# A graph layer on one core: one shared edge stream of split rows, and three node groups summed through a counted adjacency

## What is computed

```python
agg = segment_sum(x[src], dst, num_segments=6250)          # 200000 edges, rows of 256 floats
h = relu(agg @ W_rel + b_rel + x @ W_root)                 # 6250 x 512
gates = h @ W_ih.T + b_ih + b_hh                           # i, f, g, o; f is not used
c = sigmoid(i) * tanh(g)
out = layernorm(x + (sigmoid(o) * tanh(c)) @ W_fc + b_fc)  # 6250 x 256
```

## Time and profile before

| what | value |
|---|---|
| median of 3 runs | 1966.54 us (1962.2 to 1970.02) |
| profiled execution, span (the page gives no other time for it) | 2818.8 us |
| its mean granted clock of TensorE | 0.800 |
| PE busy, weight loads busy | 1874.5 us (66%), 1404.0 us (50%) |
| POOL busy, DVE busy, ACT busy | 1505.5 us (53%), 627.4 us (22%), 333.4 us (12%) |
| software queue of the gathers | 184.11 MB, 22.4% of 16 engines |
| steps gathered, pair steps counted | 345, 92 |

### The profile page before, as it was taken

How to read it: one execution, slowest core, us unless ns; L and a number is a source line. 1 busy time by engine, 2 the same in 40 slices (tenths; PEclk the granted TensorE clock), 3 DMA queues, 4 the chain that set the end, 5 groups by cost and what they waited for, 6 DMA issues and landing times.

```text
span 2818.8 us, 31563 instructions
## 1 busy us (share of the span) xinstructions
PE 1874.5 (66%) x7122; PEld 1404.0 (50%) x7123; DVE 627.4 (22%) x1236; ACT 333.4 (12%) x650; POOL 1505.5 (53%) x1774
## 2 busy tenths in 40 slices
PE   3736684857576757568568668568655765675678
PEld 0324262534445646457457457346534654554457
DVE  7411422323231211112012112112111211121112
ACT  0000020101010101001001112001101110111013
POOL 5776447364545474555654544654565547446640
PEclk9767696778778877789679789679778877887789
DMA  4333113121212232232222222322232223222220
GB/s 155 89 95 92 57 57 89 45 85 52 76 54 87 73 103 75 76 87 86 83 85 84 72 71 67 90 74 70 75 89 74 74 60 97 67 70 83 86 67 15
DMA packets 103600, 217.34 MB, mean 77 GB/s; under 512 B 37253, under 2 KB 56760, under 8 KB 103480
## 3 DMA queue, kind: packets, MB, share of 16 engines
q0 software_dynamic: 67392, 184.11, 22.4%
q10 hardware_dynamic: 32984, 25.63, 3.1%
q1 hardware_dynamic: 3202, 7.33, 0.7%
HBM read 210.58 MB, written 6.40 MB: 77 GB/s over the span
## 4 chain that ended last, share of the span: by engine, by line
PE 47%; another core or an unknown queue 26%; issue 17%; DVEq 4%; DVE 4%; ACT 1%; ACTq 0%; DMA 0%; SPq 0%
PE ps_blk L396 18%; PE ps_agg L339 16%; PE ps_y L405 3%; PE ps_blk L381 3%; PE ps_blk L383 3%; PE ps_win L320 2%; DVEq L694 1%; DVE hot_key L682 1%; DVEq L678 1%; DVE onehot L694 1%; PE ps_win L329 1%; PE ps_tr L320 1%; DVEq L690 0%; PE ps_tr L369 0%
## 5 line engine op out<-in xcount | busy, mean ns | idle before, releaser
L285 POOL DMA_INDIRECT rows<-in_x,idx x1404 | 1417.2, 1009 | 1171.6 <-issue 1098.1
L339 PE MATMUL ps_agg<-rows,onehot 128*125 x2760 | 784.4, 443 | 605.5 <-DVE onehot L694 419.3
L339 PEld LDWEIGHTS ps_agg<-rows,onehot 128*125 128x125 f32 x2760 | 580.0, 218 | 805.9 <-issue 704.6
L396 PE MATMUL ps_blk<-h_t,wih_sb 128*128 128x250 f32 x2400 | 581.1, 403 | 194.1 <-issue 115.4
L396 PEld LDWEIGHTS ps_blk<-h_t,wih_sb 128*128 128x128 f32 x2400 | 491.1, 206 | 283.7 <-issue 128.4
L694 DVE SCALAR_TENSOR_TENSOR onehot<-iota_f,tile_first,dst_f 128x500 f32 x345 | 255.4, 740 | 1276.3 <-remote 727.0
L702 DVE TENSOR_TENSOR tanh_g<-sig_i,tanh_g 128x250 f32<-128x250 f32 x100 | 42.0, 420 | 651.6 <-ACT tanh_g L507 516.2
L486 ACT ACTIVATE agg_n<-ps_agg 125x512 f32<-125x512 f32 x24 | 14.3, 597 | 1200.1 <-PE ps_agg L361 516.5
L320 PE MATMUL ps_win<-hot_key,hot_lo 128*128 x248 | 113.6, 610 | 38.5 <-DVE hot_key L682 29.2
L271 POOL COPY idx<-src_sb 128x4 int32 x352 | 81.9, 233 | 65.0 <-issue 62.8
L682 DVE TENSOR_TENSOR hot_key<-iota_h,rel 128x1960 f16 x92 | 107.8, 1171 | 0.8 <-issue 0.8
(11 more groups left out here) (106 smaller groups left out, 645.4 us busy)
## 6 DMA issues: line engine op xcount, KB each, us to landing
rows<-in_x,idx POOLq DMA_INDIRECT x1404
hot_key<-in_xb ACTq DMA_DIRECT2D x7, 896.0 KB
x_t<-in_xT ACTq DMA_DIRECT2D x50, 125.0 KB
x_n<-in_x ACTq DMA_DIRECT2D x50, 125.0 KB
out<-y ACTq DMA_DIRECT2D x50, 125.0 KB
wih_sb<-in_w_ihT SPq DMA_DIRECT2D x1, 2048.0 KB
wih_sb<-in_w_ihT SPq DMA_DIRECT2D x1, 1024.0 KB
src_sb<-in_srcT SPq DMA_DIRECT2D x1, 786.0 KB, 6.7
```

Of the source, the lines that this page charges most:

```text
L285: g.indirect_dma_start(rows[:, k * QC + j, :], None, x, bass.IndirectOffsetOnAxis(ap=idx[:, k, j:j + 1], axis=0)).then_inc(landed[k][j // ...
L339: last = mm(o, onehot[:, half * QC + j, :], rows[:, ds(slot + j, 1), :], start=False, stop=False)
L396: last = mm(o, wih_sb[:, k, col:col + P], h_t[:, k, :], start=(k == 0), stop=(k == KH - 1))
```

## The change

- **Split rows.** A prologue on DVE and SP cuts each value of `x` into a high part (low 12 bits cleared) and the rest, and writes both to a table `x_parts` in HBM, 2 KiB a row, in 10 pieces of 625 nodes. The gather reads this table. `rows` and `onehot` become float32r, and a visit multiplies 512 columns at once (high and low side by side in one PSUM bank); ACT copies the low half and DVE adds the high half (`copy_low`, `add_high`). POOL starts only when all 10 pieces are written; 5 splits stand among the first 5 windows on DVE.
- **One stream.** Tiles are taken in node order and share steps: a tile begins with the step on which the last one ended (a further **visit** of it, no further gather). By the drawn edges there are 258 steps and 301 visits in 44 tiles.
- **Ring** of 6 steps in place of 13; BANKS 3 in place of 4.
- **Three dense groups.** The first 750 nodes are counted: 75 windows with, by the drawn edges, 92 + 50 + 47 = 189 pair steps, three products of 7 batches with two `xs` buffers.
- **Order.** Five windows (37 pair steps) come before the first tile; the other 70 stand in 27 portions of 2 or 3 windows, behind the gates of j = 0, 1 and 2 (9 of the turns); the second tile comes between the gates j = 1 and j = 2; a product batch stands ahead of a gate group. On DVE a portion's windows stand ahead of the LSTM multiplies of that gate group. Turns 5, 11 and 17 have no tile.

```diff
+DENSE = 3
+EARLY_WINDOWS = 5
+HEAD_TURNS = ((3, 2, 2), (3, 2, 2), (2, 2, 2))
+WINDOW_TURNS = ((3, 3, 3), (3, 3, 2), (3, 3, 2))
+PERIOD = 6
-RING = 13
+RING = 6
-BANKS = 4
+BANKS = 3
...
-        rows = sb("rows", [P, RING * QC, D_IN])
-        onehot = sb("onehot", [P, 2 * QC, TN])
+        rows = sb("rows", [P, RING * QC, D_ROW], f32r)
+        onehot = sb("onehot", [P, 2 * QC, TN + 1], f32r)
...
+            for i in range(2):
+                pool.wait_ge(piece_out[i], 16 * X_PIECES // 2)
...
                     pool.wait_ge(steps_summed, s + 1)
                     for j in range(QC):
                         g.indirect_dma_start(
-                            rows[:, k * QC + j, :], None, x,
+                            rows_f[:, k * QC + j, :], None, x_parts,
...
+            def visit(o, s, u, half, first=False):
+                pe.wait_ge(gathered, s + (RING + 1))
+                pe.wait_ge(hot_ready, u + 1)
+                for j in range(QC):
+                    ins = mm(o, onehot[:, half * QC + j, 0:TN], rows[:, ds(slot + j, 1), :].squeeze(1), start=(first and j == 0), stop=False)
+                    if j == 0 and not first:
+                        ins.then_inc(steps_summed, 1)
+                ins.then_inc(hot_used, 1)
...
                 if t is not None:
+                    tile_sum(t, 0)
+                for j in range(KH):
+                    if j == 2 and t is not None:
+                        tile_sum(t, 1)
+                    if j in at:
+                        product_batch(k, at[j])
+                    if not first:
+                        gates(n - 1, j)
+                    if j < 3 and wins[j] > 0:
+                        windows(w, wins[j])
+                        w = w + wins[j]
...
+            def split(i):
+                dve.wait_ge(piece_in[i % 3], 16 * (i // 3) + 16)
+                if i >= 2:
+                    dve.wait_ge(piece_out[i % 2], 16 * (i // 2))
+                link(v.tensor_scalar(x_out[i % 2][:, :, 0, :].bitcast(i32), x_in[i % 3].bitcast(i32), HIGH_BITS, None, ALU.bitwise_and))
+                v.tensor_tensor(x_out[i % 2][:, :, 1, :], x_in[i % 3], x_out[i % 2][:, :, 0, :], ALU.subtract).then_inc(piece_split, 1)
...
+            def visit(t, s, u, half, first):
+                dve.wait_ge(hot_used, u + (2 if first else 1))
+                v.scalar_tensor_tensor(onehot[:, 0:QC, 0:TN] if first else onehot[:, ds(half * QC, QC), 0:TN],
...
+            def add_high(t, a):
+                dve.wait_ge(low_copied, t + (a + 1))
+                v.tensor_tensor(agg_n[:, a, :], ps_agg[a][0:TN, 0:D_IN], agg_n[:, a, :], ALU.add).then_inc(agg_evac, 1)
...
+            for i in range(EARLY_WINDOWS):
+                window(i)
+                split(5 + i)
+            first_visit(0)
```

More of the change, by code:

```diff
@@ L555, in _ @@
-            n = HEAD_TURN
-            turn(n, head, tail(n - 1), tail(n - 2))
-            turn(n + 1, tail(n), head, tail(n - 1), t=n)
-            turn(n + 2, tail(n + 1), tail(n), head, t=n + 1)
-            with act.Fori(HEAD_TURN + 3, GROUPS) as n:
-                turn(n, tail(n - 1), tail(n - 2), tail(n - 3), t=n - 1)
+            act.wait_ge(gate_bias_ready, 1)
+            windows(0, EARLY_WINDOWS, 0)
+            w = EARLY_WINDOWS
+            for n, wins in enumerate(HEAD_TURNS):
+                g = DENSE + n
+                turn(n, g, g - 1 if n >= 1 else None, g - 2 if n >= 2 else None, t=2 * n, w=w, wins=wins, node=w * WN)
+                w += sum(wins)
@@ L565, in _ @@
-            gates(n - 1)
+            store(n - 2, n - 2)
+            for j in range(KH):
+                gates(n - 1, j)
             deviation(n - 1)
-            store(n - 1, tail(n - 2))
-            act.wait_ge(y_free, 32 * GROUPS + 16)
+            store(n - 1, n - 1)
+            act.wait_ge(y_free, 16 * GROUPS)
         @block.vector
@@ L741, in normalise, with windows, turn @@
                 ins.then_inc(out_ready, 1)
-            def turn(n, back=2, t=None, begun=False, w=None, begin=None):
-                if begin is not None:
-                    tile_sum(begin, 0)
+            def windows(w, n_windows):
+                for i in range(n_windows):
+                    window(w + i if isinstance(w, int) else dve.snap(w + i, min_val=0, max_val=WINDOWS - 1))
+            def turn(n, back=2, t=None, w=None, wins=(0, 0, 0), end=False):
                 if t is not None:
-                    if back == 0:
-                        windows(w)
-                    if not begun:
-                        tile_sum(t, 0)
-                    if w is not None and back > 0:
-                        windows(w)
-                    tile_sum(t, 1)
+                    other_visits(t)
+                    first_visit(t + 1)
@@ new lines, in turn @@
+                if t is not None:
+                    other_visits(t + 1)
+                    if not end:
+                        first_visit(t + 2)
+                    add_high(t, 1)
+                if wins[2] > 0:
+                    windows(w + (wins[0] + wins[1]), wins[2])
+                if back >= 1:
+                    cell(n - 1, 2)
+                    out_gate(n - 1, 1)
+                    cell(n - 1, 3)
+                    out_gate(n - 1, 2)
+                    out_gate(n - 1, 3)
+                    norm_stats(n - 1)
```

695 lines of the change are left out of this document (397 added, 298 removed).

## The result

The changed kernel takes 2135.5 us (median of 4, 2133.9 to 2142.7) against 1965.6 (1962.2 to 1970.0) for the kernel before: a ratio of **1.087** (95% interval 1.085 to 1.090), slower. Forecast were 2010, 2.2% slower, and a range of 1890 to 2130: the side was right, the size was not, and the range was missed by 5.5 us.

A forecast was written before the change was run, and what follows sets the result against it. It took POOL's descriptors to bound the kernel from turn 5 on, PE and DVE counting before. PE's new work, 1868 us, plus 105 of row waits and 35 of clock gave 2008, predicted as 2010, 2.2% slower; range 1890 to 2130.

The forecast's parts named there:

- The turn of the bound: Whole kernel: 87 steps, 470 us, leave POOL's chain, more than PE's waits, so PE is late next.
- PE's sum: PE in the kernel before: its work adds up to 1719 us, so ordinarily it waits some 247.
- Start, 233: Start of the kernel: POOL begins near 162 us, after the last piece's write; first tile summed at 233.
- Visits, 1.27: Tiles' visits on PE: one float32r pass, with DVE's one-hots setting 1.27 us a visit; 288 visits, 366 us.
- Waits for rows, 105: PE waiting for gathered rows: 105 us in tiles 1 to 9, nothing added in later turns.
- counting behind the first tile: 152 pair steps in 27 portions: 385 us at 2.53 each, 350 after the portions' savings.
- closing matmuls: Tile borders: 44 closing matmuls of 0.21 us, 10 us in all.
- products, matrix work and the close: PE's 21 product batches, 124 us, and the unchanged matrix work with the closing 64, together 785 us.
- Clock, 35: Gates behind a portion of windows begin at a lower clock: 27 x 1.3, 35 us more.
- Rival A: PE's pieces overlap better, with visits under 1.05 us and portions hiding two pair steps: 1890 us, faster; chance 0.30.
- B: Visits: float32r passes twice, a visit takes 1.7 to 1.8 us, total time 2115 us; chance 0.10.
- C: POOL's gathers: a step of 2 KiB rows costs more; at 7 us a step, total time 2165 us; chance 0.14.

The follow-up runs named there:

- plain6: The changed kernel with the split undone: float32 rows of 1 KiB gathered from x, still six steps in the ring; 2131 us, 1.082 of the kernel before.
- plaind1: The changed kernel with unsplit float32 rows of 1 KiB, twelve steps in the ring and one dense group for three; 1901 us, 0.967 of the kernel before.
- f32r12: The changed kernel with unsplit 1 KiB rows, twelve ring steps, multiplied in one float32r pass without x's low parts; 1855 us, 0.942 of the kernel before.
- plainbest13: The changed kernel with unsplit float32 rows, thirteen ring steps, three buffers for counting's one-hots, output gate's product behind the one-hots; 1900 us, 0.965 of before.

## Why the prediction was wrong in size

**The turn of the bound: right.** PE's sum (1719 and 247 of waits) and POOL as the kernel's end led to one statement: take 87 steps from POOL, and PE is late next, with more work than before. The page after shows PE at 48% of the chain for POOL's 9, and plain6 and plaind1 say that two more dense groups cost more on PE than they save in visits, by the estimate above 85 us with an equal ring. That POOL set the end of the kernel before in an ordinary run is not shown: its only trace is from a disturbed chip. plaind1, the kernel nearest to it, has PE at 41% of the chain and POOL at 36%.

**Start, 233: 24 too low.** A split is 1.48 + 1.49 us, not 2.4, and DVE waits for the pieces' writes, 23.5 us in all ahead of the first window, which the sum had put down as "4 us of data and as much of latency" for the last one. It had taken 305 GB/s from a stretch of gathers; the pieces' queue moves 133. POOL began at 186, not 162; 13 steps and the landing took 71, as forecast (the sum's 68 + 3).

**Visits, 1.27: nearly right.** In the 14 tiles that waited neither for rows nor behind the gates a visit takes 1.30. Behind the first tile all visits together, without their waits for rows and the late one-hots, are 396 us for 366, 1.37 each: a visit whose rows come late runs at half the clock, four matmuls in 2.06 us for 1.2, with a granted clock of 0.57 between 311 and 337 us. The mechanism (one pass; PE's 0.76, DVE's 0.74 and 0.2) held, and the rivals of two passes and of dearer 2 KiB steps fell: 2.20 us for eight matmuls, and 5.1 us between steps at the start (1003 ns an indirect DMA over the whole run). For the first, the Trainium skill (FP8 and Floating Point Precision, TensorE Precision Notes) had pointed the right way. Its four passes for true FP32 agree with the runs as well: back to back, a float32 matmul of 256 columns is two records 0.215 apart in plain6, 0.43 in all, and the same matmul as float32r is 0.117 in f32r12.

**Waits for rows, 105: where the sum failed first.** For tiles 1 to 9 it had 105, and 97 are measured. Then it said "Later a turn takes 11 steps or fewer ...; nothing added", and compared a turn's sum on POOL with a turn's sum on PE, 46 against 44. Measured are 39 more, nearly all in turns 6 to 12. Both halves of the sentence were wrong. Turns 6 to 9 take 14, 12, 12 and 12 steps, by their visits. And the rows are wanted in two bursts a turn: with six slots POOL cannot work ahead through the matrix work and the windows between them, so a tile with six new steps waits some 2.6 us for the last one and a tile with seven 7 us, whatever the turn's sum is. The comparison held from turn 13 on, where a tile has five new steps or fewer (0.9 us of waits).

**One-hots of the second tile, in no term: where it failed second.** They stand behind L760 on DVE: 13 turns, 35 us. The change had moved this tile into the gates; I had costed the move by PE alone and not read what stands ahead of its one-hots on DVE.

Behind the first tile, visits, one-hots and rows so took 567 us for 471: 31 for rows (39 less the 8 that the early tiles fell short), 35 for the late one-hots, 30 for the visits.

**The rest.** Start to start on PE, counting behind the first tile took 363 (350), closing matmuls 13 (10), and products, matrix work and the close together 931 (909). *Clock, 35:* too dear; the gate matmuls are 535.5 us busy here against 520.8 in plainbest13, so about 15, and these are in the 931 already. Sum of the misses: 24 + 96 + 13 + 3 + 22 - 35 = 123 on 2008, 2131 of a span of 2132.6. So no one term carries the miss: the start, the late one-hots, the visits and the rows are 24 to 35 each, all on the same side, and a clock term that was not needed hid 35 of them.

**Rival A** (faster, 0.30) asked for visits under 1.05 and portions that hide their first pair steps. Neither came with two buffers (visits 1.30 at best). With plain rows, thirteen steps, three buffers for counting and the later output gate the kernel is faster than the one before, as plainbest13 shows, but that is another change.

**The range** ended at 2130 because each case's top was taken alone: mine at 2060, B at 2115, C at 2165 with a share of 0.14. No case had waits for rows *and* one-hots above their terms together.

## What to carry to other kernels

A ring is sized by the longest stretch in which its consumer does something else, not by the mean rates. If the producer stands idle for want of a slot and the consumer waits for rows in the same profile, look at the slots first: here six more were worth some 145 us by the estimate, and visits of half the columns 59. So a change that doubles the bytes of a slot has to be charged for the slots that it takes away, and a table that must be written first for every microsecond until its last piece. Where two engines hand buffers back and forth and each waits about 1 us a round, try a third buffer before moving the work: here it took 0.54 us off a round in a long run of rounds (37 in 66 us for 86), 0.24 in short portions, and kept the clock up as well. And when work moves to another place on one engine, read what then stands ahead of its inputs on the others.

## What the runs showed of the hardware that I had not expected

**Slow stretches on a disturbed chip.** The same program, changed kernel, on a quiet chip and on a disturbed one: weight loads in the first tile.

```profile
225.22 1.34 PEld L327 LDWEIGHTS ps_agg<-rows,onehot 128*125 128x125 f32 x4 [3.79 <-issue]
230.11 1.35 PEld L327 LDWEIGHTS ps_agg<-rows,onehot 128*125 128x125 f32 x4 [3.54 <-issue]
```

```profile
224.71 1.34 PEld L327 LDWEIGHTS ps_agg<-rows,onehot 128*125 128x125 f32 x4 [3.56 <-issue]
230.56 0.28 PEld L327 LDWEIGHTS ps_agg<-rows,onehot 128*125 128x125 f32 x1 [4.50 <-issue]
231.96 0.28 PEld L327 LDWEIGHTS ps_agg<-rows,onehot 128*125 128x125 f32 x1 [1.12 <-issue]
233.35 0.28 PEld L327 LDWEIGHTS ps_agg<-rows,onehot 128*125 128x125 f32 x1 [1.11 <-issue]
```

Up to 225 us the two agree within 0.6 us. From then on, for 49 us, the instructions of PE's sequencer on the disturbed chip take 0.70 us or come 0.70 or 1.4 apart, register arithmetic and branches too, where the quiet chip's take 0.03 to 0.21. Its records around one loop iteration (start, duration, kind, line):

```
227.02 0.70 ALU_OP         L340        quiet: 225.65 0.03
228.42 0.70 COMPARE_BRANCH L340        quiet: 225.74 0.21
229.82 0.70 FUSED_REGOPS   L340        quiet: 226.01 0.05
```

Such stretches, 5 to 50 us long as a rule, come on one engine or another, about once a turn: a turn of the tail takes 62 to 72 us for 46 to 49, but turns 5 and 17, with no tile and no windows, take 31.3 on either. Those that show in register instructions (three or more of 0.6 us and over, close together) are 21 in the kernel before, 20 of them on POOL, its latest engine, some 345 us in all; in the changed kernel 22, 16 on DVE and 6 on PE, some 345 as well. They do not account for the whole difference, 852 us in the kernel before and 546 in the changed kernel: others show only in the pace of other instructions, and what the rest is stays open. Why some chips have them, no run tells.

The two stalls of the earlier trace rows I had misread. POOL's, up to 1527.69, has no slow instruction in it; it ends as PE takes up steps again at 1524.99, behind the matrix work of that turn, and looks like the plain wait for a free slot. DVE's, from 1546.9 to 1574.5, goes with such a stretch on PE, up to 1562.4: its weight loads, 0.21 apart before, come mostly 1.4 apart here. The 12 us after it stay open.

```profile
1548.35 0.18 PEld L339 LDWEIGHTS ps_agg<-rows,onehot 128*125 128x125 f32 x1 [1.17 <-issue]
1549.77 0.28 PEld L339 LDWEIGHTS ps_agg<-rows,onehot 128*125 128x125 f32 x1 [1.24 <-issue]
1551.17 0.28 PEld L339 LDWEIGHTS ps_agg<-rows,onehot 128*125 128x125 f32 x1 [1.12 <-issue]
```

The cadences, on which the sum was built, come from stretches with no slow instruction and were right.

**The clock in the gates behind short visits.** In f32r12 a visit's matmuls are over in 0.5 us at best and PE waits for one-hots between visits (98 us in all, against 30 in plain6). The granted clock in the gates behind a tile of the tail is then 0.90, against 1.00 in plain6:

```profile
1681.00:1692.00 11.00, 11.00 (x49) 9.69 (x48) 3.07 (x10) 4.01 (x7) 8.83 (x11) 0.90 0.38 106
```

```profile
1952.00:1963.00 11.00, 11.00 (x54) 9.78 (x54) 3.18 (x10) 4.01 (x7) 8.67 (x13) 1.00 0.34 99
```

and the same 48 gate matmuls take 10.9 to 12.0 us for 10.3, in the tail's 14 tiles some 17 us more. That eats what the shorter visits save there: the 14 tiles themselves take 104 us against 114 in the changed kernel, as DVE's one-hots set the pace of both. So the kernel with half the columns has a tail no shorter than the changed one.
